# The bulk loads of an attention stage issued by ScalarE instead of SyncE, and X in three groups

## The reference

```python
def reference(x, itok, cond, L0_w, Wq, Wk, Wv, Wo):
    # layer 0: w = L0_w[itok] is (32, 128, 128), it mixes the 128 tokens
    x = x + einsum('bct,bcd->bdt', x, L0_w[itok])
    # layer 1: attention over the 128 tokens
    q, k, v = (einsum('bsd,ed->bse', x, W) for W in (Wq, Wk, Wv))   # 16 heads of 64
    q = q * minimum(cond, 4.0)
    scores = einsum('bhqd,bhkd->bhqk', q, k) / 8
    attn = softmax(where(causal, scores, finfo.min))
    out = einsum('bhqk,bhkd->bhqd', attn, v)
    return x + einsum('bsd,ed->bse', out, Wo)
```

## Time and profile before

| | us |
|---|---|
| median of 3 runs | 1646.51 (1646.39 to 1650.28) |
| profiled execution | 1646.84 |
| its span, first to last instruction | 1645.5 |
| PE busy | 1582.5 (96%) |
| ACT busy | 817.6 (50%) |
| DVE busy | 987.1 (60%) |
| POOL busy | 850.2 (52%) |
| mean granted PE clock | 0.984 |

### The profile page before, as it was taken

How to read it: one execution, slowest core, us unless ns; L and a number is a source line. 1 busy time by engine, 2 the same in 40 slices (tenths; PEclk the granted TensorE clock), 3 DMA queues, 4 the chain that set the end, 5 groups by cost and what they waited for, 6 DMA issues and landing times.

```text
span 1645.5 us, 23425 instructions
## 1 busy us (share of the span) xinstructions
PE 1582.5 (96%) x7563; PEld 1323.8 (80%) x7563; DVE 987.1 (60%) x1752; ACT 817.6 (50%) x2221; POOL 850.2 (52%) x748
## 2 busy tenths in 40 slices
PE   9999999999999999899998889999999989999999
PEld 7888888888887888788787777877887767888887
DVE  5835454443576677677675667666776645555553
ACT  6645555541565666466565456555666532222221
POOL 2454555452455555566564555555565434555552
PEclk9999999999999999999999999999999999999999
DMA  9867887757766656555778565565564687545442
GB/s 324 312 239 271 293 313 289 253 209 250 253 205 200 190 191 196 162 163 173 193 199 239 170 184 160 165 173 170 157 178 122 220 297 264 179 154 173 172 161 83
DMA packets 192811, 341.46 MB, mean 208 GB/s; under 512 B 23986, under 2 KB 112306, under 8 KB 186546
## 3 DMA queue, kind: packets, MB, share of 16 engines
q1 hardware_dynamic: 192690, 339.98, 63.7%
HBM read 184.70 MB, written 134.22 MB: 194 GB/s over the span
## 4 chain that ended last, share of the span: by engine, by line
PE 74%; DMA 8%; SPq 8%; issue 3%; ACT 3%; POOL 2%; DVE 2%; ACTq 0%; DVEq 0%; POOLq 0%
PE p_PJ L690 16%; PE p_PJ L691 16%; PE p_PJ L692 16%; PE p_SC L692 5%; PE p_SC L690 5%; PE p_SC L691 5%; DMA t_XL<-xtl_scratch 4%; SPq L1498 4%; PE p_PV L797 3%; ACT t_PP L1010 1%; PE p_PV L690 1%; POOL t_VV L1299 1%; PE p_PV L692 1%; PE p_PV L691 1%; PE p_LP L690 1%
## 5 line engine op out<-in xcount | busy, mean ns | idle before, releaser
L690 PE MATMUL p_PJ<-t_XH,t_WH 128*128 128x512 f32 x1008 | 402.2, 399 | 37.1 <-DMA t_XL<-xtl_scratch 34.4
L691 PE MATMUL p_PJ<-t_XL,t_WH 128*128 128x512 f32 x1008 | 400.6, 397 | 0.0
L692 PE MATMUL p_PJ<-t_XH,t_WL 128*128 128x512 f32 x1008 | 398.4, 395 | 0.0
L1010 ACT ACTIVATE t_PP<-t_PP,t_st 128x128 f32<-128x128 f32 x512 | 199.5, 391 | 186.2 <-DVE t_st L1183 184.7
L690 PEld LDWEIGHTS p_PJ<-t_XH,t_WH 128*128 128x128 f32 x1008 | 193.9, 192 | 76.6 <-issue 31.4
L1305 POOL TENSOR_TENSOR t_PP<-t_PP,t_st 128x512 f32<-128x512 f32 x128 | 133.2, 1041 | 218.4 <-DVE t_st L1187 218.4
L692 PEld LDWEIGHTS p_PJ<-t_XH,t_WL 128*128 128x128 f32 x1008 | 193.1, 192 | 42.0
L1199 DVE TENSOR_REDUCE t_AT<-p_PV 64x256 f32<-64x512 f32 x256 | 174.0, 680 | 78.9 <-ACT t_AC L1025 59.1
L691 PEld LDWEIGHTS p_PJ<-t_XL,t_WH 128*128 128x128 f32 x1008 | 194.1, 193 | 33.0
L1311 POOL TENSOR_TENSOR t_AT<-t_AT,t_AC 128x256 f32<-128x256 f32 x128 | 122.0, 953 | 129.4 <-DVE t_AT L1199 129.4
L1308 POOL TENSOR_TENSOR t_PS<-t_PT,t_PS 128x512 fp32r<-128x512 f32 x122 | 157.7, 1293 | 19.4 <-ACT t_PS L1017 19.4
(11 more groups left out here) (252 smaller groups left out, 3538.4 us busy)
## 6 DMA issues: line engine op xcount, KB each, us to landing
t_XH<-xth_scratch SPq DMA_DIRECT2D x56, 512.0 KB, 5.0
t_XL<-xtl_scratch SPq DMA_DIRECT2D x56, 512.0 KB, 5.7
t_PT<-t_TB SPq DMA_DIRECT2D x580, 32.0 KB, 1.9
v_scratch<-t_VR SPq DMA_DIRECT2D x64, 256.0 KB, 4.3
xth_scratch<-t_XH SPq DMA_DIRECT2D x16, 1024.0 KB, 4.0
xtl_scratch<-t_XL SPq DMA_DIRECT2D x16, 1024.0 KB, 6.4
t_VX<-v_scratch SPq DMA_DIRECT2D x32, 512.0 KB, 7.2
at_scratch<-t_AT SPq DMA_DIRECT2D x128, 128.0 KB, 4.3
```

The source lines that it names most:

```text
L690: pe.matmul(bank, lh, rh, start=first, stop=False, skip_group_check=goes_on)
L691: pe.matmul(bank, lh, rl, start=False, stop=False, skip_group_check=goes_on)
L692: return pe.matmul(bank, ll, rh, start=False, stop=last, skip_group_check=goes_on)
L1010: act.activation(PP[:, u, h, :], PP[:, u, h, :], ACT.Exp, bias=st[:, 0, u, h:h + 1], scale=1.0, accum_out=st[:, 1, u, h:h + 1]).then_inc(a ...
```

## The change

ACT issues X (all stages), V from stage 1 on, the weights n = 2 and 3 with their first columns, and Wo; the DMAs then run on ACT's own hardware queue. They stand in `act_program` behind the exps of the same quarter step and ahead of `t_PS`. SP keeps the P moves, the stores, V of stage 0 and the weights n = 0 and 1. X is planned in three groups, at steps 3.5, 4 and 4.5, at 19.5, 20 and 20.5, and at 35.5 and 36 of stage j-1; V at 36.5. For j = 1 (pieces every five steps from 12) and j = 9 (every four from 24) the steps of X stay. The waits ahead of each load are the same as before, now in ACT's order. The values of the last cell come two steps later. In the pair part, the first sum of pair 0 waits for the last P move instead of the last attention stores; its fourth sum, which writes `AT`, waits for those.

```diff
@@ -389,7 +389,7 @@
-                    v = a + (25.25 + 3.25 * k if last else 29 + 4.5 * k)
+                    v = a + (27.25 + 3.25 * k if last else 29 + 4.5 * k)
...
-                    X_load.put(t0 - STEPS + (12 + 5 * i if j == 1 else 24 + 4 * i if j == NG + 1 else (1, 6, 17, 22, 33, 38, 49, 54)[i]), (j, i))
+                    X_load.put(t0 - STEPS + (12 + 5 * i if j == 1 else 24 + 4 * i if j == NG + 1 else (3.5, 4, 4.5, 19.5, 20, 20.5, 35.5, 36)[i]), (j, i))
             for k in range(2):
-                V_load.put(t0 + (-11, 2.75)[k] if j == 0 else t0 - STEPS + (28 if j == 1 else 10), (j, k))
+                V_load.put(t0 + (-11, 2.75)[k] if j == 0 else t0 - STEPS + (35 if j == 1 else 36.5), (j, k))
...
+        def act_load_W(n, part):
+
+            cols = W_COLS[part]
+            for low in range(2):
+                if n == 2 and part == 1 and low == 0:
+                    act.wait_ge(pe_q, 4 * NG)
+                elif n == 3 and part == 1 and low == 0:
+                    act.wait_ge(pe_k, 4 * NG)
+                to = (WH, WL)[low][n % 2][:, :, cols].bitcast(f32)
+                act.dma_start(to, qk_half(n, low, cols)).then_inc(l_W[n][part], 16)
+
+        def act_load_W1():
+
+            act.wait_ge(s_p, 32 * 32)
+            act.wait_ge(pe_k, 4 * (NG - 1))
...
+        def act_load_X(j, i):
+
+            z, g = x_at_(j), GROUP[j]
+            if i == 0 and j == 1:
+                act.wait_ge(pe_P, 7 * (NP - 2))
+                for n in range(2):
+                    act.wait_ge(s_xt[n], 32 * NG)
+            elif i == 0 and j == NG + 1:
+                act.wait_ge(pe_k, 4 * NG + 1)
+            elif i == 0:
+                act.wait_ge(pe_k, 4 * (j - 1))
+            low, cols = i % 2, slice(1024 * (i // 2), 1024 * (i // 2) + 1024)
+            to = (XH, XL)[low][z][:].bitcast(f32).rearrange("p d t -> p (d t)")[:, cols]
+            act.dma_start(to, (xth_d, xtl_d)[low][g][:, cols]).then_inc((l_XH, l_XL)[low][z], 16)
+
+        def act_load_V(j, k):
+
+            act.wait_ge(pool_vl, GB * j)
...
+        def act_load_wo(k, low):
...
         def act_program():
...
+                for _ in W1_load(tick):
+                    act_load_W1()
+                for j, i in X_load(tick):
+                    act_load_X(j, i)
+                for j, k in V_load(tick):
+                    if j:
+                        act_load_V(j, k)
+                for n, part in W_load(tick):
+                    if n >= 2:
+                        act_load_W(n, part)
+                for k, low in O_fetch(tick):
+                    act_load_wo(k, low)
                 for P in half_at(tick):
...
                             pool.wait_ge(s_O, 32 * 32)
-                            for k in range(2):
-                                pool.wait_ge(s_at[k], 16 * 64)
+                            pool.wait_ge(l_P, 160 * 64)
                         pool.tensor_tensor(sums(0), a21, a22, ALU.add).then_inc(pool_S, 1)
...
                     else:
+                        if q == 0:
+                            for k in range(2):
+                                pool.wait_ge(s_at[k], 16 * 64)
                         pool.tensor_tensor(sums(3), a12, sums(1), ALU.subtract).then_inc(pool_S, 1)
...
-                for _ in W1_load(tick):
-                    sp_load_W1()
-                for j, i in X_load(tick):
-                    sp_load_X(j, i)
                 for j, k in V_load(tick):
-                    sp_load_V(j, k)
+                    if j == 0:
+                        sp_load_V(k)
                 for n, part in W_load(tick):
-                    sp_load_W(n, part)
+                    if n < 2:
+                        sp_load_W(n, part)
...
-                for k, low in O_fetch(tick):
-                    sp_load_wo(k, low)
```

More of the change, by code:

```diff
@@ L940, in act_v_out, with qk_half @@
             act.activation(v_slot(n), bank[:], ACT.Copy).then_inc(act_v, 1)
+        def qk_half(n, low, cols):
+            return (wh_d, wl_d)[low][n].rearrange("p (d e) -> p d e", d=DC)[:, :, cols]
+        W_COLS = (slice(0, 128), slice(128, 256), slice(256, 512))
+        def act_load_W(n, part):
[7 more added lines that the diff above has]
+                act.dma_start(to, qk_half(n, low, cols)).then_inc(l_W[n][part], 16)
@@ new lines, in act_load_W1 @@
+        def act_load_W1():
+            act.wait_ge(s_p, 32 * 32)
+            act.wait_ge(pe_k, 4 * (NG - 1))
+            for n in range(2):
+                for low in range(2):
+                    to = (XH[0], XL[0])[low][:, :, 128 * n:128 * n + 128].bitcast(f32)
+                    act.dma_start(to, qk_half(2 + n, low, slice(0, 128))).then_inc(l_W1, 16)
+        def act_load_X(j, i):
+            z, g = x_at_(j), GROUP[j]
+            if i == 0 and j == 1:
+                act.wait_ge(pe_P, 7 * (NP - 2))
+                for n in range(2):
+                    act.wait_ge(s_xt[n], 32 * NG)
[6 more added lines that the diff above has]
+            act.dma_start(to, (xth_d, xtl_d)[low][g][:, cols]).then_inc((l_XH, l_XL)[low][z], 16)
@@ new lines, in act_load_V @@
+        def act_load_V(j, k):
+            act.wait_ge(pool_vl, GB * j)
+            cols = slice(1024 * k, 1024 * k + 1024)
+            act.dma_start(VX[:, 2 * k:2 * k + 2, :].rearrange("p u e -> p (u e)"), v_d[j // NG][GROUP[j]][:, cols]).then_inc(l_V[k], 16)
+        def act_load_wo(k, low):
+            if k == 3 and not low:
+                act.wait_ge(s_O, 32 * 32)
+                act.wait_ge(pool_vl, GB * NGRP)
+            if k == 1:
+                act.wait_ge(pe_pv, 16 * (NGRP - 1))
+            elif k in (0, 2):
+                act.wait_ge(pe_q, 64)
+            elif k != 3:
+                act.wait_ge(pe_k, 64)
+            act.dma_start(wo_tile(k)[low].bitcast(f32).rearrange("p d e -> p (d e)"), (woh_d, wol_d)[low][k]).then_inc(l_O[k], 16)
@@ L1412, in sp_store_qk @@
             sp.dma_start(wl_d[m // 8][:, cols], low.bitcast(f32)).then_inc(s_p, 16)
-        def qk_half(n, low, cols):
-            return (wh_d, wl_d)[low][n].rearrange("p (d e) -> p d e", d=DC)[:, :, cols]
         def sp_load_W(n, part):
-            cols = (slice(0, 128), slice(128, 256), slice(256, 512))[part]
+            cols = W_COLS[part]
             for low in range(2):
@@ L1525, in sp_store_wo @@
             sp.dma_start(wol_d[k][:, cols], OL[:].bitcast(f32)).then_inc(s_O, 16)
-        def sp_load_wo(k, low):
-            if k == 3 and not low:
-                sp.wait_ge(s_O, 32 * 32)
-                sp.wait_ge(pool_vl, GB * NGRP)
-            if k == 1:
-                sp.wait_ge(pe_pv, 16 * (NGRP - 1))
-            elif k in (0, 2):
-                sp.wait_ge(pe_q, 64)
-            elif k != 3:
-                sp.wait_ge(pe_k, 64)
-            sp.dma_start(wo_tile(k)[low].bitcast(f32).rearrange("p d e -> p (d e)"), (woh_d, wol_d)[low][k]).then_inc(l_O[k], 16)
         def sp_load_pair(q):
```

39 lines of the change are left out of this document (6 added, 33 removed).

## The result

The changed kernel takes 1633.05 us (median of 11 runs, 1626.61 to 1642.44); the kernel before, run beside it, 1648.36 us (median of 11, 1644.2 to 1655.16). The ratio is 0.9905, with a 95% interval of 0.9883 to 0.9928. So it is faster, by 0.9%. The forecast was 1582, and the range ended at 1606: the result lies 27 us outside, inside the third rival's 1600 to 1640.

The account below looks back on a forecast made before the run. It took PE as the bound, losing time to standing and low clock. Terms -55.4 + 0 + 2 - 2.3 + 2 - 1.5 - 3 - 8 + 2 = -64.2 on a 1645.5 us span gave 1581.3, forecast as 1582 us; range 1570 to 1606.

Parts of the forecast that it names:

- third rival: Ordinary cells: bulk groups make small transfers late, 1 us over the slack in 30 cells; 1610 us; chance 0.13 over 1600-1640.
- new contention, +2: P moves and stores beside a group of X: delays mostly held by the slack; +2 us (0 to +30).
- X, -55.4: The 13 stage starts: waits for late X go, 37 us of standing and 18 of low clock.
- ACT pays 0 for X: ACT's idle gap before the exps hides the X and V issues, median 0.43 us each; cost 0.
- slack of 2.3 us: ACT's cover behind the gap, around KH, KL and the scores, meant to hold 1.7 us of store delay.
- The -1.5: Early P move at 428.39, landing after 6.52 us behind X pieces: small transfers leave the bulk behind, -1.5 us.
- The terms (+2, -2.3, +2): Later weights on ACT: first columns +2, next four between exps -2.3 net, stage 8's X and two weight pairs +2.
- The -3: Cell around 1300 us, where Wo loads stood on the same queue: 3 of its 4.7 us come back.
- the -8: End of the kernel: Wo on ACT's queue and last values two steps later gain 8 us (-3 to -9.4).
- the prediction's own sign for its second rival: At the end: the last out store still takes 7 us to land.
- second rival: The second queue saves issuing time only, so 12.5 us of small-transfer gains are lost; 1595 us; chance 0.13.

Follow-up runs that it names:

- one: The changed kernel, but from stage 3 on each X piece moves 64 bytes a row, with the issues kept: 1607.02 us, ratio 0.9772.
- two: The changed kernel with only X on ACT, in groups; V, later weights, Wo and the last values as before, on SP: 1616.62 us, 0.9827.
- Six: The changed kernel with X and V in single pieces at the steps of before, and X of stage 1 on SP: 1601.88 us, 0.9719.
- Five: The changed kernel with X and V in single pieces at the steps of before, later weights and first columns on SP: 1606.82 us, 0.9755.
- nine: As kernel seven, all on SP, with second-half weights early in single pairs and X of stage 9 at kernel seven's steps: 1590.86 us, 0.9646.
- ten: As Six, with nine's early weights and earlier X steps for stage 9: 1590.2 us, 0.9648.
- kernel seven: All loads on SP as before the change, X in single pieces at earlier steps, last values at 25.25: 1602.55 us, 0.9729.

## Why the prediction was wrong

The step that failed is **new contention, +2**. Its place was named (P moves and stores beside a group of X), but the size and the path were wrong: a loss over the slack in 30 cells was put at the end of the range, and it is what happened: the term measured 22.6 us. It is the largest of four misses. The sum by stretches, from the terms of the prediction laid on the account of before:

| stretch | before | forecast | after | missed |
|---|---|---|---|---|
| first four | 0.4 | -1.1 | 7.8 | 8.9 |
| turn | 16.4 | 9.7 | 18.1 | 8.4 |
| ordinary | 51.7 | 3.7 | 24.3 | 20.6 |
| tail | 324.7 | 316.7 | 326.8 | 10.1 |

The stretches' misses make 48.0, of 48.2 between the forecast span of 1581.3 and 1629.5.

*X, -55.4: right.* No wait for X is left, and the low clock went with it: the cells across the old waits take 13.33 us. *ACT pays 0 for X: right*, shown by one, where the issues stay and the cost goes. The median issue is 0.34 to 0.45 us and the gap of 3.3 us held four.

*New contention: wrong by 20.6.* The estimate rested on a store that loses "as much again", 3.4 us, halved to 1.7 without a row for the halving. The stores beside the third group lose about 4 us (7.9 and 7.4 us, where they take 3.4 and 3.2 in the next cell), more than the whole 3.4. V's two pieces, which make that group 2 MB, stood in no term of contention; two without them costs nothing there. What follows from one late move to the next, through `t_PS`, `t_TB` and the stores issued behind them, is likely but was not followed step by step. The attention stores, which hold DVE's reduction and by it PE's `p_PV`, stood in no term at all, though they landed in 4.2 us already in the kernel before. The slack of 2.3 us that was to take it up was the one ahead of the scores; the path that ended last goes through `p_PV`.

*First four: wrong by 8.9.* The -1.5 assumed that a move gains when X leaves its queue. Six shows what X of stage 1 does on a queue of its own: it takes the DMA engines from weights that are needed first.

*Turn: wrong by 8.4.* The terms (+2, -2.3, +2) priced how long ACT is held, and that is the mechanism of the kernel after. The cell of the first columns was forecast at 2 us and cost 1.7. The four weights between the exps were forecast at 5.7 us in place of the old 8.0, and cost 6.7 (842.97 above). The two pairs and X in stage 8 were forecast at 2 us and cost 7.4 (891.59 above): this is the term that was mis-sized. The other 2.3 us are two cells behind late stores, one of which was issued at 853.85 and landed 9.30 us later; no term had them. Five shows that with SP as issuer ACT is free and the loss comes by SP's queue, nine and ten that spacing takes most of it away.

*End: wrong by 10.1.* The -3 came, the -8 did not. PE's wait for the last values fell from 6.0 us to 3.6, but a new one of 4.7 us for `t_AT` stands at the values before them, and the granted clock over the 57 us from 1304.9 is 0.88, where it was 0.94 before. The out store at 1323.29 takes 8.0 us to land: the prediction's own sign for its second rival. The reading of the earlier trace rows, an out store late because Wo stood ahead of it, led to the idea that another queue frees it. With two queues the DMA share is still 0.89, and there what is small lands late on its own queue as well.

The rivals: the second was right in what it says of the small transfers (its rule held at the end and for X), but took the -55.4 for sure with no cost beside it. The third was the case for the ordinary cells: it named 28 us there, where 20.6 came. That the total lies in its range is in part luck, since the other stretches, which it didn't price, brought 27.4. It had 0.13, since the forecast's slack was believed. The first four cells and the turn had no rival of their own.

## What to carry to other kernels

A second issuing queue is no second set of DMA engines: it removes the order between transfers, so what is needed later can overtake what is needed now. If a load is late because its issue is late, move its issue earlier on the queue it has, one piece at a time (kernel seven, -2.7%, without a new queue). Keep such loads small and apart: 1 MB at once cost nothing here, 2 MB did. Weight loads of many short rows hold the engine that issues them when they are bunched, whichever it is. Before bulk loads are put together, look up which small transfers stand beside them, who waits for those, and add up their delays along the chain to the bounding engine, not one by one.
